# LSTM pass 3 of a graph network kernel: sixteen tiles of 8 batches or twelve of 12 and 8, and each pass as one list of tiles

## What is computed

```python
h = relu(einsum('ts,bsh->bth', adj, x @ Wg0 + bg0))
h = relu(einsum('ts,bsh->bth', adj, h @ Wg1 + bg1))
for p in range(1, 5):
    nw = 128 // p
    wins = h[:, :nw * p, :].reshape(B * nw, p, H)      # windows of p steps
    last = lstm_last(Wih[p-1], Whh[p-1], bih[p-1], bhh[p-1], wins)
    h = h.at[:, arange(nw) * p + (p - 1), :].set(last)  # the window's last step
# one LSTM step, p of them in a window, starting from h = c = 0:
g = x_t @ Wih.T + h @ Whh.T + bias                     # i, f, g, o
c = sigmoid(f) * c + sigmoid(i) * tanh(g);  h = sigmoid(o) * tanh(c)
```

## Time and profile before

| what | value |
|---|---|
| median of 3 runs | 875.0 us (874.92 to 875.27) |
| span of the profiled execution | 876.8 us, 15203 instructions |
| TensorE busy | 856.3 us, 98% |
| VectorE busy | 698.4 us, 80% |
| ScalarE busy | 607.1 us, 69% |
| GpSimd busy | 237.5 us, 27% |

### The profile page before, as it was taken

The page is one execution under the profiler, slowest core; times in us unless marked ns, Lnnn a source line. Parts: engine busy times, 40 slices in busy tenths (PEclk is TensorE's granted clock), DMA queues, the critical chain, the costliest instruction groups (busy, mean ns, idle before and its releaser), DMA issues.

```text
span 876.8 us, 15203 instructions
## 1 busy us (share of the span) xinstructions
PE 856.3 (98%) x5228; PEld 744.9 (85%) x5228; DVE 698.4 (80%) x1572; ACT 607.1 (69%) x1117; POOL 237.5 (27%) x562
## 2 busy tenths in 40 slices
PE   8999999999999999999999999999999999999996
PEld 7888888878778789999998887878887999999885
DVE  5888888868888878777777777767987787897986
ACT  3778878886766766767676666666896677776454
POOL 0233333340000000000000001003474355666766
PEclk9999999999999999999999999999999999999999
DMA  4222221000000001000000086777155010111223
GB/s 139 74 61 61 61 61 49 1 1 1 1 1 0 1 1 49 1 1 1 1 2 0 12 180 145 163 167 154 45 125 117 14 37 26 37 38 37 59 64 84
DMA packets 30988, 45.43 MB, mean 52 GB/s; under 512 B 2593, under 2 KB 23745, under 8 KB 27841
## 3 DMA queue, kind: packets, MB, share of 16 engines
q1 hardware_dynamic: 27680, 27.34, 10.8%
q0 software_dynamic: 2304, 16.78, 9.4%
q10 hardware_dynamic: 928, 0.35, 0.2%
HBM read 19.29 MB, written 8.39 MB: 32 GB/s over the span
## 4 chain that ended last, share of the span: by engine, by line
PE 79%; DVE 13%; ACT 4%; issue 2%; DMA 1%; POOL 1%; DVEq 0%; POOLq 0%; ACTq 0%
PE psum L505 7%; PE psum L506 7%; PE psum L507 7%; PE psum L523 6%; PE psum L519 6%; PE psum L520 6%; PE psum L1344 5%; PE psum L1266 5%; PE psum L412 3%; PE psum L454 3%; PE psum L1357 3%; PE psum L388 2%; PE psum L389 2%; PE psum L387 2%; PE psum L1324 2%
## 5 line engine op out<-in xcount | busy, mean ns | idle before, releaser
L646 ACT ACTIVATE work<-psum,bias 128x512 f32<-128x512 f32 (+1 forms) x408 | 232.1, 622 | 27.4 <-PE psum L523 26.0
L505 PE MATMUL psum<-hT_hi,w_hi 128*128 128x512 f32 (+1 forms) x406 | 148.2, 365 | 3.3 <-ACT work L646 2.8
L506 PE MATMUL psum<-hT_lo,w_hi 128*128 128x512 f32 (+1 forms) x406 | 146.5, 361 | 0.0
L507 PE MATMUL psum<-hT_hi,w_lo 128*128 128x512 f32 (+1 forms) x406 | 146.4, 361 | 0.0
L627 ACT ACTIVATE work<-work 128x512 f32<-128x512 f32 (+1 forms) x112 | 63.8, 570 | 108.9 <-DVE work L967 71.9
L978 DVE TENSOR_TENSOR work<-work 128x512 f32<-128x512 f32 (+1 forms) x111 | 68.6, 618 | 54.0 <-ACT work L627 54.0
L519 PE MATMUL psum<-hs_hi,w_hi 128*128 128x512 f32 (+1 forms) x288 | 103.9, 361 | 1.1 <-DVE hs_hi L912 0.9
L523 PE MATMUL psum<-hs_lo,w_hi 128*128 128x512 f32 (+1 forms) x288 | 104.5, 363 | 0.0
L520 PE MATMUL psum<-hs_hi,w_lo 128*128 128x512 f32 (+1 forms) x288 | 103.2, 358 | 0.0
L1172 POOL DMA_DIRECT2D hT_lo<-hT_hi x8 | 7.5, 937 | 351.3 <-DVE hT_lo L914 330.8
L505 PEld LDWEIGHTS psum<-hT_hi,w_hi 128*128 128x128 f32 x406 | 76.4, 188 | 17.4 <-ACT work L646 5.2
(11 more groups left out here) (225 smaller groups left out, 1902.9 us busy)
## 6 DMA issues: line engine op xcount, KB each, us to landing
work<-x_by_batch SPq DMA_DIRECT2D x32, 256.0 KB, 2.7
x_stage<-x_by_state SPq DMA_DIRECT2D x8, 1024.0 KB, 5.6
hT_lo<-hT_hi POOLq DMA_DIRECT2D x8, 1024.0 KB, 9.8
hT_lo<-x_stage POOLq DMA_DIRECT2D x8, 1024.0 KB, 7.2
out<-x_kept SPq DMA_DIRECT2D x31, 256.0 KB, 2.3
work<-L_gnn_Wih SPq DMA_DIRECT2D x4, 256.0 KB, 2.9
work<-L_gnn_Whh SPq DMA_DIRECT2D x3, 256.0 KB, 3.1
out<-x_kept SPq DMA_DIRECT2D x2, 128.0 KB, 2.3
```

The source lines that it names most:

```text
L505: pe.matmul(out, w_hi[:, w, g, :], xh, start=True, stop=False)
L506: pe.matmul(out, w_hi[:, w, g, :], xl, start=False, stop=False)
L507: mm = pe.matmul(out, w_lo[:, w, g, :], xh, start=False, stop=(t == 0))
L646: op = act.activation(gate[s][g][:, 0:ph.width], psum[:, 4 * s + g, 0:ph.width], ACT.Tanh if g == G else ACT.Sigmoid, bias=bias[:, b:b + 1])
```

## The change

`LstmPhase` gets a list of tile sizes in batches instead of a size and a number of pairs, and the pass before it. Pass 1, 2 and 4 keep their sizes (4, 8 and 16). Pass 3 gets twelve tiles: 12, 8, 12, 8, 12, 8, 12, 8, 12, 12, 12, 12. A 12-batch tile is 12 x 42 = 504 columns wide. The loops over iterations are gone from all engines: a pass is one list of pairs, so `pending` and `before` carry over everywhere but at the end of a pass. What the first step of a tile waits for is worked out from the sizes (`covering`: how many tiles of the pass below hold so many batches).

```diff
-    def __init__(self, p, batches, pairs, n_batch, items_before, f_before, tiles_before):
-        self.p, self.batches, self.pairs = p, batches, pairs
+    def __init__(self, p, sizes, before):
+        self.p, self.sizes = p, sizes
         self.windows = P // p
-        self.width = batches * self.windows
-        self.iters = n_batch // (batches * 2 * pairs)
-        self.per_iter = 2 * p * pairs
...
+        self.tiles = len(sizes)
+        self.items, self.forgets = p * self.tiles, (p - 1) * self.tiles
...
+    def width(self, tile):
+        return self.sizes[tile] * self.windows
+
+    def blocks(self, tile):
+        first = sum(self.sizes[:tile]) // BT
+        return slice(first, first + self.sizes[tile] // BT)
+
+    def covering(self, batches):
+
+        return next(n for n in range(1, self.tiles + 1) if sum(self.sizes[:n]) >= batches)
...
-        for pair in range(self.pairs):
+        for pair in range(self.tiles // 2):
...
-    for p, batches, pairs in ((1, 4, 4), (2, 8, 2), (3, 8, 2), (4, 16, 2)):
-        phases.append(LstmPhase(p, batches, pairs, n_batch, items, forgets, tiles))
+    for p, sizes in ((1, [4] * (n_batch // 4)), (2, [8] * (n_batch // 8)), (3, [12, 8] * 4 + [12] * 4), (4, [16] * (n_batch // 16))):
+        assert sum(sizes) == n_batch and len(sizes) % 2 == 0
+        phases.append(LstmPhase(p, sizes, phases[-1] if phases else None))
...
-    def windows_at(ph, view, it, tile, t):
-        blocks = ph.batches // BT
-        first = (it * (2 * ph.pairs) + tile) * blocks
-        return view[:, first:first + blocks, t:t + (ph.windows - 1) * ph.p + 1:ph.p, :]
+    def windows_at(ph, view, tile, t):
+        return view[:, ph.blocks(tile), t:t + (ph.windows - 1) * ph.p + 1:ph.p, :]
...
         for ph in phases[1:]:
-            for it in range(ph.iters):
-                def from_input(tile, t, k):
-                    n = it * ph.per_iter + (ph.items_before + k)
-                    pe.wait_ge(S["gates_read"], n + (CREDIT - 1))
+            def from_input(tile, t, k):
+                n = ph.items_before + k
+                pe.wait_ge(S["gates_read"], n + (CREDIT - 1))
+                if t == 0:
+                    below = ph.before
+                    pe.wait_ge(S["tiles_done"], below.tiles_before + below.covering(sum(ph.sizes[:tile + 1])) + CREDIT)
...
-                    if k + 1 < ph.per_iter and (k + 1) % (2 * ph.p) < 2:
-                        pending = k
+                if k + 1 < ph.items and (k + 1) % (2 * ph.p) < 2:
+                    pending = (tile, k)
+                else:
+                    tanh_of(tile, k)
...
-                if before and not (ph is phases[-1] and it == ph.iters - 1):
+            if before and ph is not phases[-1]:
                     split(*before)
```

More of the change, by code:

```diff
@@ L490, in run_tensor @@
         for ph in phases[1:]:
-            for it in range(ph.iters):
-                def from_input(tile, t, k):
-                    n = it * ph.per_iter + (ph.items_before + k)
-                    pe.wait_ge(S["gates_read"], n + (CREDIT - 1))
-                    if t == 0:
[L496 to L546, removed]
-                        if j == EPS_ROWS_AT:
-                            pe.wait_ge(S["gates_read"], ph.items_before + j + (CREDIT - 1))
-                            eps_to_rows()
[L550 to L554, removed]
-                    if is_last(ph, it, k):
-                        pe.wait_ge(S["gates_read"], ph.items_after - 1 + CREDIT)
-                        entry.query(pe)
-                    if t > 0:
-                        from_state(k, forgets)
@@ new lines, in from_state @@
+            def from_state(tile, k, forgets):
+                n = ph.items_before + k
+                s = k % 2
+                hh, hl = hs_hi[:, s, 0:ph.width(tile)], hs_lo[:, s, 0:ph.width(tile)]
+                w = piece_of[ph.p - 1, 1]
+                pe.wait_ge(S["h_hi"], n - 1)
+                for g in (F, I, G, O):
+                    out = psum[:, 4 * s + g, 0:ph.width(tile)]
+                    pe.matmul(out, w_hi[:, w, g, :], hh, start=False, stop=False)
+                    pe.matmul(out, w_lo[:, w, g, :], hh, start=False, stop=False)
+                    if g == F:
+                        pe.wait_ge(S["h_done"], ph.f_before + forgets)
+                    pe.matmul(out, w_hi[:, w, g, :], hl, start=False, stop=True).then_inc(gate_psum[g], 1)
@@ L987, in leave_state @@
+            if before and ph is not phases[-1]:
+                split(*before)
     def leave_state(dve):
         ph = phases[-1]
+        w = ph.width(ph.tiles - 1)
         dve.wait_ge(S["tanh_ready"], ph.items_after)
-        dve.tensor_tensor(h_full[1][:, 0:ph.width], gate[1][O][:, 0:ph.width], tanh_c[1][:, 0:ph.width], ALU.mult).then_inc(S["h_mul"], 1)
+        dve.tensor_tensor(h_full[1][:, 0:w], gate[1][O][:, 0:w], tanh_c[1][:, 0:w], ALU.mult).then_inc(S["h_mul"], 1)
     def leave_halves(dve, s):
@@ L1024, in back @@
     RING = LAG + 9
-    GROUP = before.phases[-1].batches // BT
+    GROUP = before.phases[-1].sizes[0] // BT
     LAST = tiles + LAG + 3
```

316 lines of the change are left out of this document (177 added, 139 removed).

## The result

| | time, median (range) | ratio to before, 95% interval |
|---|---|---|
| before | 875.13 us (874.92 to 877.73, 4 runs) | |
| the change | 866.01 us (865.78 to 866.13, 4 runs) | 0.9887 (0.9866 to 0.9907) |

The change is 9.1 us faster. The forecast was 867.4 us with a range of 864.6 to 870.4: right, and 1.4 us too careful, which is less than the interval on the ratio leaves open (0.002 of 875 is 1.8 us). In a second measurement, among the experiments, the change took 866.6 us, ratio 0.9894 (0.9875 to 0.9913).

What follows compares the result with a forecast made beforehand. TensorE, busy 98% of the span, was taken as the bound, with waits where pairs of tiles change. Gains of 0.3 + 5.8 + 1.5 = 7.6 us took the 875.0 us median to 867.4 us, range 864.6 to 870.4.

Steps and rivals of the forecast that it cites:

- Part 1: Pass 3 on TensorE: fewer, wider matmuls, 138.4 us against 138.7, 0.3 us less; bounds 2.7 less to 1.5 more.
- my upper bound: Pace of 504-wide matmuls in pass 3, scaled from pass 4's 512-wide pace: 0.235 us for inputs, 0.226 for state.
- rival 2: Wide matmuls in pass 3 at the lower bound, 0.220 and 0.225: 2.4 us better, 865.0 us; chance 0.13.
- Part 2: Waits inside pass 3, at its entry and where pairs of tiles change: 5.8 us less.
- The walk through a change of pair: Pass 3, narrow tile to wide: cover grows 0.71, ScalarE's chain 0.44, so a 0.17 us wait becomes 0.10 slack.
- The entry: From pass 2 into pass 3: order kept, waits shrink by 0.27 and 0.23, in all 0.5 less of 2.29 us.
- Rival 1: Waits stay at four of pass 3's five changes of pair, 0.51 us each: 869.4 us; chance 0.17.
- Part 3: Passes 2 and 4 lose their iterations: pass 2 1.5 us less (between 0.5 and 2.0), pass 4 taken as 0.
- Part 4: Work off the path (ScalarE, VectorE, GpSimd, SyncE's loads): none of it bounds the kernel; no gain or loss priced.
- Rivals 3 and 4: Rival 3: nothing comes through, 875.0 us, chance 0.03; rival 4: wide tile starves beside narrow, 878.6 us, chance 0.02.

Runs made afterwards that it cites:

- e1: The change with pass 3 back at sixteen 8-batch tiles, the single list kept: 872.04 us, ratio 0.9954.
- e5: The change with the held back tanh and split also carried over the ends of passes 2 and 3: 866.52 us, ratio 0.9875.
- e2: The change with the iteration ends put back in passes 2 and 4 alone: 868.76 us, ratio 0.9934.
- e7: The change with pass 3 as eight pairs of a 12-batch and a 4-batch tile: 881.7 us, one run.
- e9: The change with the 8-batch tile ahead of the 12-batch tile in the four mixed pairs: 868.04 us, ratio 0.9922.
- the carry again: Second measurement of e5 (the carry), the change with held back work carried over the ends of passes 2 and 3: 867.27 us, ratio 0.9896.
- e3: The change with the iteration ends put back in passes 2, 3 and 4, its widths kept: 870.14 us, ratio 0.9943.
- e8: The change with pass 3 as five pairs of 12-batch tiles and one last pair of 4-batch tiles: 880.6 us, one run.
- e4: The change with pass 3's same twelve tiles reordered, the four narrow (12 and 8) pairs last: 866.93 us, ratio 0.9892.
- e6: The change with held back work carried over the ends of passes 2 and 3 and the 12 and 8 pairs last: 866.71 us, ratio 0.9888.
- e10: The change with the 8-batch tile first in mixed pairs and held back work carried over the passes' ends: 868.67 us, ratio 0.9914.

## Why the prediction was right, point by point

- **Part 1, pace.** Forecast 0.229 and 0.2255 for wide inputs and state; over the whole pass they were 0.2249 and 0.2278. A wide tile took 12.89 us and not 12.97, and all tiles 137.9: 1.2 us less and not 0.3. The state's 0.2278 lies above my upper bound of 0.226, and the inputs' 0.2249 a third of the way up from the lower one, so rival 2, both at the lower bound, didn't come. The mis-sized term is the inputs': their measured pace lies midway between pass 3's own 336-wide row carried on (0.220) and what I took from the 512-wide passes (0.229). One price per column doesn't hold in all three: over its columns an input start costs 0.015 in pass 3 at 504, 0.019 in pass 2 and 0.025 in pass 4, there with the DMA engines idle too; that the step between windows is the reason was not tested. The flat 2.5 ns of the Trainium skill (TensorE: Matmul & The Clock Gate, Back-to-back issue gap) would be worth 0.6, half of what was measured; the rows give an extra over columns that grows from 11 to 14 ns at 336 to 15 to 18 ns at 504.
- **Part 2, waits in pass 3.** Forecast 5.8 less, measured 8.3 - 2.0 = 6.3. The walk through a change of pair held: no wait for an engine at the first four, and 0.2 us lost at the last; what is left is the entry's 1.36 and some 0.4 at the epsilon matmuls. The entry was mis-sized, 0.9 less and not 0.5. Rival 1 did not occur, and e1 shows why it was a rival: narrow tiles do keep 0.5 each. The walk let each VectorE instruction grow by at most 0.234; the cast of a wide last tile grew by 0.34.
- **Part 3.** Pass 2 forecast 1.5 less, measured 2.28, outside its bounds of 0.5 to 2.0. The failed step: "so each of three is worth 0.52". I measured one end, the last, and took the two that carry table work to be worth no more; they were worth 0.9 each, since VectorE's late split stood there too, ahead of the state at the first and ahead of the table work at the second. Pass 4 forecast 0, measured 0.39 more: the end gave 0.48 as forecast, the widths took 0.87, most of it at the entry, and not at most 0.5. I had counted only the wait for ScalarE there; what showed is a wait for the state's high half, which the slow cast makes later.
- **Part 4** held as far as the trace shows: TensorE's waits late in pass 4 (1.1 and 0.8 us over pace) are the same in both kernels. Rivals 3 and 4 were not seen; even 12 batches beside 4 did not starve.
- **The sum.** 7.6 forecast, 9.36 in the passes, 9.1 in the medians. Three terms were too careful (0.9, 0.5, 0.8) and one too hopeful (0.4). That the total came so near is owed in part to the last, which took back some of the others.

## What to carry to other kernels

Where two tiles alternate on TensorE, price a change of tiles as cover against chain: the cover is the matmuls of the tiles that follow, the chain the gates, tanh and split of the tile before. Where widths are mixed, try the narrow tile last in a pair and avoid a wide one ahead of a mixed pair. Remove the boundary in the engines' lists first: it was worth 0.76 us at each end between 336-column tiles, about 0.5 beside 504, and 0.5 to 0.9 at 512. Read each instruction of the chain at its own shape and place, since one cast took 0.67 us where its neighbours in width took 0.43. Look at every instance of a wait before multiplying one by a count.

## What the runs showed of the hardware beyond that

**The clock behind a wait.** Behind the passes stands the attention part, the same in all these kernels, yet that stretch took 258.9 to 262.2 us. Table by stretch, TensorE, at its first softmax wait; the kernel before, then the change, then e5:

```profile
665.00:669.00 4.00, 2.26 (x21) 0.98 0.49 98
669.00:673.00 4.00, 4.00 (x27) 0.59 0.82 164
```

```profile
654.00:658.00 4.00, 2.27 (x22) 1.00 0.49 98
658.00:662.00 4.00, 3.96 (x33) 1.00 0.81 164
```

```profile
652.00:656.00 4.00, 2.28 (x23) 1.00 0.04 8
656.00:660.00 4.00, 4.00 (x24) 0.57 0.81 164
```

The same 2.3 busy us of 4 come before each, with one wait of 1.7 us in them. Then the granted clock falls or doesn't. A second such place lies some 217 us behind the passes, with 2.4 busy us of 4; in the change's own profile it fell there, to 0.91 and 0.66 over 820 to 828. The fourteen profiled executions sort by how often it fell: not at all, 258.9 us (e2, e7, e9); at one place, 260.2 to 260.5 (the change both times, the carry again, e1, e3, e8); at both, 262.1 to 262.2 (before, e4, e5, e6, e10). So each fall costs about 1.6 us.

Where the clock stays up elsewhere, the mean clock of an execution tells roughly which it was: 0.997 for none, 0.996 for one, 0.994 for both. The change had 0.995 to 0.998 in ten of ten executions. The two measurements of the carry had 0.992 to 0.994 in eight of ten (866.01 to 867.50 us), and 0.996 to 0.997 in the other two (862.79 and 864.56). So the carry's 1.6 us are real in the passes and mostly given back behind them. Why its clock falls more often, or whether it does beyond chance, stays open: no run moved that wait by itself. No version tried is faster than the change by more than the noise.

**The start.** The 1.7 us ahead of pass 2 arise in the first 20 us, beside the first loads: the record has 88 matmuls there in the kernel before, e1 and e4, and 100 in the change, e5 and e6. e4 and e6 share their tiles and the code up to there, so it isn't the edit. The rows show the lower clock level. In the kernel before, matmuls of 512 columns start 0.43 apart at 10.57 and 11.00, which is 512 columns at 1.2 GHz; in the change, 0.23 apart at 9.47 and 9.70. The column of the granted clock says 1.00 for both. In e10, where the same matmuls also start 0.43 apart (10.62 and 11.05), it has the lower level on record; TensorE by stretch:

```profile
10.00:11.00 1.00, 1.00 (x4) 0.50 0.54 61
```

So TensorE left the lower level at some 8 us in the change and near 13 us in the kernel before. What decides when is open; the other profiled executions lie at one of these two or between them.
